# Two fields looked up by TensorE, rows fetched by SyncE, and scores in four column tiles: a change to an attention factorization machine on Trainium2

## The reference

```
B, N_DENSE, N_FIELDS, VOCAB, EMBED_DIM, ATT_DIM = (2048, 13, 26, 12500, 32, 8)
FIRST, SECOND = np.triu_indices(N_FIELDS, k=1)
emb = jax.vmap(lambda tbl, idx: tbl[idx], in_axes=(0, 1), out_axes=1)(embed_tables, sparse)
bi = emb[:, FIRST, :] * emb[:, SECOND, :]
a = jax.nn.relu(jnp.einsum('bpd,dh->bph', bi, att_w_w) + att_w_b)
scores = jnp.einsum('bph,ho->bpo', a, att_d_w) + att_d_b
att_weight = jax.nn.softmax(scores, axis=1)
att_out = jnp.sum(att_weight * bi, axis=1)
x = jnp.concatenate([att_out, dense], axis=-1)
out = jax.nn.sigmoid(x @ fin_w + fin_b)
```

## Time and profile before

| | |
|---|---|
| median of 3 executions | 534.23 us (533.74 to 535.23) |
| the profiled execution | 534.63 us, its span 532.8 us |
| POOL busy | 384.7 us (72%), 400 gathers |
| PE busy | 371.2 us (70%) |
| DVE busy | 278.7 us (52%) |
| ACT busy | 123.5 us (23%) |
| TensorE's granted clock, mean | 0.922 of full speed |

### The profile page before, as it was taken

How to read it: one execution, slowest core, us unless ns; L and a number is a source line. 1 busy time by engine, 2 the same in 40 slices (tenths; PEclk the granted TensorE clock), 3 DMA queues, 4 the chain that set the end, 5 groups by cost and what they waited for, 6 DMA issues and landing times.

```text
span 532.8 us, 6246 instructions
## 1 busy us (share of the span) xinstructions
PE 371.2 (70%) x1940; PEld 120.4 (23%) x1940; DVE 278.7 (52%) x434; ACT 123.5 (23%) x301; POOL 384.7 (72%) x404
## 2 busy tenths in 40 slices
PE   0468748788836776686946686786874678687694
PEld 0122211222312321121222221121231222112121
DVE  4144544555654455545754446455765445454674
ACT  0000012322520112222540011232442001122253
POOL 5777777777777777777777777777777777777720
PEclk9998998998969999989987999889996999788998
DMA  8223222122112222222112222322111222212210
GB/s 228 36 12 14 15 13 13 15 15 12 16 12 13 12 13 13 14 13 14 13 13 13 13 13 13 13 14 13 14 13 13 12 13 12 13 13 13 14 6 1
DMA packets 13828, 9.96 MB, mean 19 GB/s; under 512 B 6781, under 2 KB 13437, under 8 KB 13565
## 3 DMA queue, kind: packets, MB, share of 16 engines
q0 software_dynamic: 12800, 6.58, 21.1%
q1 hardware_dynamic: 730, 2.98, 2.2%
q10 hardware_dynamic: 288, 0.28, 0.2%
HBM read 9.81 MB, written 0.01 MB: 18 GB/s over the span
## 4 chain that ended last, share of the span: by engine, by line
POOL 65%; issue 21%; PE 7%; DVE 2%; DMA 2%; ACT 1%; POOLq 0%; DVEq 0%; ACTq 0%
POOL emb L250 65%; PE sums_f L303 2%; PE back_s L267 2%; PE first L294 2%; DMA emb<-tables,rows 1%; PE sums_s L314 1%; DMA par<-params 1%; ACT expd L441 0%; PE back_f L326 0%; ACT expd L415 0%; DVE onehot L506 0%; DVE second_f L551 0%; PE turned L286 0%; DVE neg_max_early L539 0%; POOLq L94 0%
## 5 line engine op out<-in xcount | busy, mean ns | idle before, releaser
L250 POOL DMA_INDIRECT emb<-tables,rows x352 | 337.2, 958 | 107.3 <-issue 107.0
L522 DVE TENSOR_TENSOR ring<-emb_t,turned 128x512 f32<-128x512 f32 (+9 forms) x180 | 193.8, 1113 | 212.1 <-PE turned L286 190.6
L303 PE MATMUL sums_f<-ring,par 128*32 128x512 f32 (+1 forms) x672 | 163.7, 634 | 0.0
L267 PE MATMUL back_s<-onehot,look_table 125*128 125x512 f32 x200 | 106.5, 671 | 58.1 <-DVE onehot L506 58.1
L294 PE MATMUL first<-ring,par 128*32 128x512 f32 (+1 forms) x672 | 107.6, 635 | 1.7 <-DVE ring L522 1.7
L382 ACT ACTIVATE hidden<-first,par 128x512 f32<-128x512 f32 (+1 forms) x84 | 56.4, 675 | 184.2 <-PE first L294 163.4
L314 PE MATMUL sums_s<-hidden,par 128*32 128x512 f32 x168 | 91.8, 637 | 2.9 <-ACT hidden L382 2.9
L286 PE MATMUL turned<-par,emb 128*128 128x128 f32 x100 | 31.5, 320 | 85.8 <-DMA emb<-tables,rows 64.4
L375 ACT ACTIVATE emb_t<-turned 128x128 f32<-128x128 f32 x100 | 27.6, 276 | 189.2 <-DVE ring L522 175.8
L267 PEld LDWEIGHTS back_s<-onehot,look_table 125*128 125x128 f32 x200 | 38.5, 207 | 115.3 <-DVE onehot L506 88.6
L250 POOL DMA_INDIRECT emb<-tables,rows_first x48 | 47.3, 986 | 18.7 <-issue 14.3
(11 more groups left out here) (50 smaller groups left out, 89.5 us busy)
## 6 DMA issues: line engine op xcount, KB each, us to landing
emb<-tables,rows POOLq DMA_INDIRECT x352, 3.3
look_table<-tables SPq DMA_DIRECT2D x1, 1400.0 KB
look_index<-look_ids SPq DMA_DIRECT2D x1, 1024.0 KB, 8.4
emb<-tables,rows_first POOLq DMA_INDIRECT x48, 3.6
par<-params ACTq DMA_DIRECT2D x1, 265.0 KB, 3.3
ids<-sparse SPq DMA_DIRECT2D x1, 208.0 KB, 2.7
look_table<-tables SPq DMA_DIRECT2D x1, 162.5 KB
feats<-dense SPq DMA_DIRECT2D x1, 104.0 KB, 2.8
```

The source lines that it names most:

```text
L250: pool.indirect_dma_start(emb[:, f, g * D:(g + 1) * D], None, stacked, bass.IndirectOffsetOnAxis(ap=row, axis=0),).then_inc(gathered[f], 16)
L267: nc.tensor.matmul(back_s[:].rearrange("p c b -> p (c b)"), look_table[:, c, :], onehot[0:LOOK_PARTS, c % ONEHOT, :], start=c == 0, stop=c ...
L303: mm = nc.tensor.matmul(sums_f[j * TILE:(j + 1) * TILE, 0:pairs_c(gr) * P], fin[:, e, :], ring[:, gr % RING, 0:pairs_c(gr), j, :], start=e ...
L522: nc.vector.tensor_tensor(slot[:, at:at + n, :], emb_t[:, i:i + n, :], turned[f % 2][:, 0:P].unsqueeze(1).broadcast_to((P, n, P)), ALU.mul ...
```

## The change

1. **Two fields are looked up**, 6 and 15. Field 6 takes five chunks at each of fields 1 to 5, field 15 three at each of fields 6 to 13 and one at 14. `look_rows` of the second runs on VectorE between the mask of field 6 and the products of field 6. SyncE loads the second table when the first is in. TensorE waits for a table at its first look-up, and no longer ahead of its first transpose.
2. **Chunk numbers lie in PSUM**: `look_chunk` is now a view of the bank `back_f`, so the one-hots read PSUM.
3. **Six tiles of field 21 are fetched by SyncE**, one row at a time (128 rows a tile, 768 transfers). It loads 16 row numbers into registers, issues 16 transfers of one row, and waits at a tile's end. One tile each for quads 0 and 1, two each for quads 2 and 3. The rows go to `emb_placed`, and ScalarE copies them into `emb` ahead of its work on field 20. GpSimd fetches the other two tiles of the placed ones at field 13 of the first quad.
4. **Scores in batches**: the score products of up to four groups stand together, each in its own column tile. Batches end at groups 3, 7, 11, 15, 17, 18 and 20. Groups lie in the banks in another order (`place`).
5. **The last field**: transpose, then first products, scores and finals of groups 18 to 20 in a written-out order; scores go back before finals.
6. `RING` 10 to 6, `HIDDEN` 4 to 6.

```diff
-RING = 10
-HIDDEN = 4
-LOOK = 10
+RING = 6
+HIDDEN = 6
+BATCH = 4
+ROWS_SP = 16
+SP_FIELD = 21
+TILES_SP = (1, 1, 2, 2)
+PLACED = 2
+SP_PLACE = 20
+SP_FIRST = 13
+LOOK = (6, 15)
+LOOK_STEP = (5, 3)
-LOOK_STEP = 3
...
+    looks_of = {f: [] for f in range(F)}
+    for n, (end, step) in enumerate(zip(LOOK, LOOK_STEP)):
+        start = LOOK[n - 1] if n else 1
+        assert (end - start) * step >= LOOKS
+        for c in range(LOOKS):
+            looks_of[start + c // step].append((n, c))
...
+    batch_ends = [gr for gr in range(GROUPS) if gr == GROUPS - 1 or
+                  gr % BATCH == BATCH - 1 and gr < FULL * GROUPS_B or
+                  gr > FULL * GROUPS_B and gr in (GROUPS - 4, GROUPS - 3)]
...
+    def place(gr):
+
+        return gr % BATCH * 2 + gr % GROUPS_B // BATCH
...
+        look_chunk = back_f[:].rearrange("p c b -> p (c b)")
...
+            stacked = tables.rearrange("f v d -> (f v) d")
+            sp.wait_ge(sp_rows_ready, 1)
+            tiles = 0
+            for q in range(QUADS):
+                for i in range(PLACED - TILES_SP[q], PLACED):
+                    t = q * G + G - PLACED + i
+                    for p in range(0, P, ROWS_SP):
+                        _, at = nc.values_load_multi_w_load_instructions(
+                            sp_rows[t:t + 1, p:p + ROWS_SP], engines=(mybir.EngineType.SP,), min_val=0,
+                            max_val=F * V - 1, skip_runtime_bounds_check_because="rows are clamped to their table")
+                        for k in range(ROWS_SP):
+                            sp.dma_start(emb_placed[p + k:p + k + 1, q, i * D:(i + 1) * D],
+                                         stacked[bass.ds(at[k], 1), :]).then_inc(sp_gathered, 16)
+                    tiles += 1
+                    sp.wait_ge(sp_gathered, tiles * P * 16)
+                sp.sem_inc(sp_quads_ready, 1)
...
-                def score_products(gr):
-                    n, c = gr // GROUPS_B, gr % GROUPS_B // 2
-                    pe.wait_ge(relu_done, q * GROUPS + (gr + 1))
+                def score_products(batch):
+                    first_gr, end = batch_ends[batch - 1] + 1 if batch else 0, batch_ends[batch]
+                    n = first_gr // GROUPS_B
+                    pe.wait_ge(relu_done, q * GROUPS + (end + 1))
...
+                    for gr in range(first_gr, end + 1):
+                        tile, half = place(gr) // 2, place(gr) % 2
+                        cut = slice(0, pairs_c(gr) * P)
+                        mm = nc.tensor.matmul(sums_s[tile * TILE:(tile + 1) * TILE, cut], d_sel[:, half, :],
+                                              hidden[:, gr % HIDDEN, cut], start=half == 0,
+                                              stop=half == 1 or gr >= FULL * GROUPS_B, skip_group_check=True)
+                    mm.then_inc(scores_done, 1)
...
+                transpose_step(F - 1)
+                score_products(BATCHES - 3)
+                first_products(GROUPS - 3)
+                final_products(GROUPS - 3)
+                score_products(BATCHES - 2)
+                first_products(GROUPS - 2)
+                first_products(GROUPS - 1)
+                final_products(GROUPS - 2)
+                score_products(BATCHES - 1)
+                final_products(GROUPS - 1)
+                scores_back(FULL)
                 finals_back(FULL)
-                scores_back(FULL)
...
+                def place_rows():
+                    act.wait_ge(placed_gathered, (QUADS * PLACED - sum(TILES_SP)) * 16)
+                    act.wait_ge(sp_quads_ready, q + 1)
+                    of_quad = emb_placed[:].rearrange("p q d -> p (q d)")[:, bass.ds(q * (PLACED * D), PLACED * D)]
+                    nc.scalar.activation(emb[:, SP_FIELD, PLACED_COLS], of_quad, ACT.Copy).then_inc(placed, 1)
...
+                    if f + 1 in LOOK:
+                        n = LOOK.index(f + 1)
+                        mask_looked(n)
+                        if n + 1 < len(LOOK):
+                            look_rows(n + 1)
```

More of the change, by code:

```diff
@@ L162, in attention_fm @@
         rows_ready = sem("rows_ready")
+        sp_ids_in = sem("sp_ids_in")
+        sp_steps = sem("sp_steps")
+        sp_rows_ready = sem("sp_rows_ready")
+        sp_gathered = sem("sp_gathered")
+        sp_quads_ready = sem("sp_quads_ready")
+        placed_gathered = sem("placed_gathered")
+        placed = sem("placed")
         gathered = [sem(f"gathered{f}") for f in range(F)]
         transposed = sem("transposed")
-        look_table_in = sem("look_table_in")
-        look_index_in = sem("look_index_in")
+        look_table_in = [sem(f"look_table_in{n}") for n in range(len(LOOK))]
+        look_index_in = [sem(f"look_index_in{n}") for n in range(len(LOOK))]
         look_steps = sem("look_steps")
@@ L242, in _ @@
                         pool.wait_ge(rows_ready, 1)
+                    if q == 0 and f == SP_FIRST:
+                        for n in range(QUADS):
+                            for i in range(PLACED - TILES_SP[n]):
+                                t = n * G + G - PLACED + i
+                                pool.indirect_dma_start(
+                                    emb_placed[:, n, i * D:(i + 1) * D], None, stacked,
+                                    bass.IndirectOffsetOnAxis(ap=rows[:, t, SP_FIELD:SP_FIELD + 1], axis=0),
+                                ).then_inc(placed_gathered, 16)
                     if q:
                         pool.wait_ge(transposed, (q - 1) * F + f + 1)
-                    for g in range(G):
+                    for g in range(G - PLACED if f == SP_FIELD else G):
                         if q == 0 and f < FIRST_FIELDS:
@@ L280, in transpose_step @@
                 def transpose_step(f):
-                    if f == LOOK:
-                        return select_step()
-                    pe.wait_ge(gathered[f], (q + 1) * (16 * G))
+                    if f in LOOK:
+                        return select_step(LOOK.index(f))
+                    pe.wait_ge(gathered[f], (q + 1) * (16 * (G - PLACED if f == SP_FIELD else G)))
+                    if f == SP_FIELD:
+                        pe.wait_ge(placed, q + 1)
                     if f >= 2:
@@ L338, in _ @@
                 transpose_step(1)
-                for f in range(1, F):
+                for f in range(1, F - 1):
                     done = groups_of(f)
                     for gr in done:
-                        if gr == done[-1] and f + 1 < F:
-                            for c in looks_of(f):
-                                look_up(c)
+                        if gr == done[-1] and f + 1 < F - 1:
+                            for n, c in looks_of[f]:
+                                look_up(n, c)
                             transpose_step(f + 1)
                         first_products(gr)
-                        if gr:
-                            score_products(gr - 1)
+                        if gr - 1 in batch_ends:
+                            score_products(batch_ends.index(gr - 1))
                         final_products(gr)
@@ L353, in _ @@
                             scores_back(gr // GROUPS_B - 1)
-                    if not done and f + 1 < F:
-                        for c in looks_of(f):
-                            look_up(c)
+                    if not done:
+                        for n, c in looks_of[f]:
+                            look_up(n, c)
                         transpose_step(f + 1)
-                score_products(GROUPS - 1)
+                transpose_step(F - 1)
[9 more added lines that the diff above has]
+                scores_back(FULL)
                 finals_back(FULL)
-                scores_back(FULL)
         @block.scalar
@@ L400, in finals_home @@
                     whole = GROUPS_B if n < FULL else END_GROUPS - 1
-                    mv = nc.scalar.activation(pairs_of(final, n * GROUPS_B, whole), finals_in_bank(0, whole), ACT.Copy)
+                    mv = nc.scalar.activation(pairs_of(final, n * GROUPS_B, whole),
+                                              finals_in_bank(every if n < FULL else end_whole), ACT.Copy)
                     if n == FULL:
                         end = final[:, :, (GROUPS - 1) * PAIRS_G:].rearrange("p g (c j) -> p g c j", j=COL_TILES)
-                        mv = nc.scalar.activation(end, finals_in_bank(whole, 1)[:, 0, :, 0:LAST_C, :], ACT.Copy)
+                        mv = nc.scalar.activation(end, finals_in_bank(end_last)[:, 0, :, 0:LAST_C, :], ACT.Copy)
                     mv.then_inc(final_done, 1)
```

142 lines of the change are left out of this document (83 added, 59 removed).

## The result

The changed kernel takes **589.1 us** (median of 4 runs, 582.77 to 590.84) against 534.05 for the kernel before: a ratio of 1.10, 95% interval [1.0963, 1.1038]. The forecast was 574 in a range of 545 to 625. The profiled execution has a span of 586.9 us.

What follows compares the result with a forecast made beforehand. The prediction took each quad's chain through TensorE and VectorE, 138.4 us against GpSimd's 118, as the bound. Start 17.2, first quad 131.9, three of 138.4 and end 7.5 gave span 571.8, forecast 574 us, range 545 to 625.

Steps and rivals of the forecast that it cites:

- own chain: Time a quad would take without waits for gathered rows: forecast to rise from 108.2 to 138.4 us, above GpSimd's 118.
- rival 1: GpSimd stays the bound because all added TensorE waits are hidden: quad chain 121, kernel 506 us; chance 0.07.
- rival 2: SyncE's rows come late, ScalarE waits at field 20 of the last quad: 664 us, half-way 618; chance 0.14.
- (c): At field 6, VectorE's row work for the second field makes TensorE idle about 5.2 us instead of 1.5: +3.7.
- (e): At fields 10 to 14 TensorE now waits for one-hots; with 0.5 for fields 7 to 9, +7.4 us a quad.
- rival 3: Half the new TensorE-VectorE turns are hidden, costing 7 instead of 14.3: quad chain 131.2, kernel 545 us; chance 0.08.
- rival 4: Four batched score products don't overlap, 3.4 us instead of 0.88: quad chain 145.6, kernel 603 us; chance 0.05.
- (a): 25 more look-ups on TensorE in each quad, 0.89 us each: +22.3 us.
- (b): One-hots read chunk numbers in PSUM, delaying TensorE 0.2 us in each turn; fields 2 to 5: +0.8 us.
- (d): After the idling at field 6, TensorE's look-ups run at a lower granted clock: +2.1 us a quad.
- (g): Batched score products save 11.2 us a quad on TensorE; 4 come back in fields 15 to 24, as VectorE limits.
- The base of 108.2: Starting point of the quad sum: the old kernel's third quad, 124.7 us, without its 16.5 us wait for gathered rows.

Runs made afterwards that it cites:

- e2: The changed kernel with one looked-up field (10, three chunks a field) instead of two; 521.4 us, ratio 0.976 to the kernel before.
- e3: The changed kernel with VectorE making a field's one-hots ahead of its wait for the transpose, not after the products; 512.5 us.
- e8: The kernel before, with one-hots made ahead of the wait for the transpose and nothing else changed; 534.5 us, ratio 1.001.
- e4: The changed kernel with the chunk numbers in SBUF instead of PSUM; 573.9 us, ratio 1.073 to the kernel before.
- e5: The changed kernel with one score product after each group (19 and 20 still together) instead of batches; 593.0 us.
- e1: The changed kernel with all tiles of field 21 fetched by GpSimd and no one-row transfers by SyncE; 585.1 us.

## Why the prediction was right, point by point

- **The mechanism held.** A quad's own chain became longer than GpSimd's 118 us, and GpSimd's saving was hidden. e2 (without the second set), e3 (without the turns) and e8 (without the turns where GpSimd binds) show the three sides of it.
- **The rivals.** The quads are 143.5 us apart and not 118 (rival 1), no engine waits for SyncE's rows (rival 2), and the waits of (c) and (e) count in full (rival 3). Four score products start 0.85 us before what follows them (386.65 to 387.50), no more than one took before, so they overlap, against rival 4; but its other half, a lower clock, is what came: 0.90 in the third quad where it was 0.93.
- **GpSimd, 94 gathers a quad, through at 481 us:** 477.6 measured, 3 us earlier; the sum had left out that one-hots from PSUM don't slow the gathers (e4).
- **(a) look-ups:** 4.41 us for five in e3, 0.88 each against 0.89.
- **(b) PSUM source:** taken 0.2 us, measured 0.25 (742 ns against 491), e4: 12 us of waits against 11.
- **(c) field 6:** 5.2 us of idling forecast, 5.12 measured.
- **(d) the clock after it:** 2.1 taken, 2.27 measured (5.11 for 2.84). But two more dips in each quad from the second on were not in the sum, at field 13 (2.7 us with what follows) and in the last field (1.6).
- **(e) turns at fields 10 to 14:** forecast 2.2, 0.5, 0.65, 2.6, 0.9; measured 2.39, 0.67, 0.74, 2.79 and none for the last, since at field 14 a batch of scores stands ahead of the look-up too.
- **(g) scores** is the step that was mis-sized. Forecast -7.2 net a quad; at an equal clock it was -3.9 (e5, first and third quad). Of the 11.2 saved on TensorE 7.3 came back, not 4, and a little more than my bound of 7: TensorE's waits in the third quad are 35.0 us with batches and 30.4 with single scores, 4.6 more, and the rest is not placed. VectorE is close to the bound of fields 15 to 24: in the changed kernel its products of two fields stand 0.34 us apart, for ScalarE's copy of the field before.

```profile
412.24 3.15 DVE L637 TENSOR_TENSOR ring<-emb_t,turned 128x1152 f32<-128x1152 f32 x2 [0.34 <-ACT emb_t L470]
```

- **The base of 108.2** was too long. I had taken the waits for rows out of the quad and left in the clock dips behind two of them. The kernel before: a field with its group after a wait of 3.1 us for rows, one after 2.9, and one without a wait.

```profile
332.10:336.60 4.50, 4.41 (x19) 0.92 (x19) 2.08 (x2) 0.96 (x2) 3.58 (x4) 0.67 0.29 13
347.80:352.20 4.40, 4.37 (x20) 1.06 (x20) 2.48 (x2) 0.69 (x1) 3.18 (x5) 0.67 0.09 11
325.70:328.70 3.00, 3.00 (x21) 0.82 (x20) 2.11 (x3) 1.24 (x3) 2.27 (x3) 1.00 0.23 13
```

That is 2.9 us that a chain without these waits doesn't have.
- **Where the 15 us are.** The start was 1.4 us later (18.6 instead of 17.2; the transposes waited for gathered rows and not for the table, as the earlier trace rows already says), the end 1.4 shorter. The first quad took 131.4 us where 131.9 was forecast, the other three 143.6 instead of 138.4: 5.2 x 3 = 15.6 us. In the third quad the terms give +3.3 for (g), +2.7 and +1.6 for the two new dips, +0.6 for the deeper dips at fields 1 and 6 and -2.9 for the base, together 5.3 of the 5.1 measured. So the good hit in the first quad was luck: (g) and the base were off by 3 us each, in opposite directions, and the new dips were not there. Why the dips came and went stays open.
- **SyncE:** 0.507 us a row against 0.6 taken and a limit of 0.64. The lower bound, 0.46 on its own queue, was nearer than my middle. The page Runtime: NRT & Kernel Launch of the Trainium skill gives about 200 ns for each register loaded, section Instruction fetch mechanics; worked out from it, a row would take 0.66, an estimate. The page speaks of loads from HBM, and these are from SBUF: the 0.507 leaves at most 0.05 for each register, so for these loads the measurement decides against it.
- **RING and HIDDEN:** no wait for a ring slot is in the trace of the changed kernel.

## What to carry to other kernels

Before a bound is lowered, work out how far below it the next one lies: here GpSimd's 126 us a quad covered a chain of 108, and a change that took 8 us from the one and added 35 to the other lost. A chain worked out by taking waits away still holds the slow stretch that followed them: read the granted clock behind each wait before it is taken out. A chain that passes back and forth between two engines isn't seen in their busy shares (TensorE 73%, VectorE 66%); it is seen in short waits of each for the other, once per step, and it may fall to a change of order that costs nothing. Measure such an edit where it binds: one-hots ahead gave 0 in the kernel before, 77 us in the changed one.

## What the runs showed of the hardware

- GpSimd's gathers slow down beside VectorE's one-hots from SBUF and not beside those from PSUM: 1.10 us for a gather that overlaps one-hots in e4 against 0.94 for one that doesn't, 976 against 946 ns in the mean of e4 and the changed kernel, 12 us in 378 gathers. The page VectorE: DVE Perf Modes of the Trainium skill, section Why PSUM operands drop a tier, says that the fast fp32 mode uses both SBUF read ports and PSUM has one; the one-hots' 491 ns from SBUF and 742 from PSUM agree. That GpSimd is held up by just this was not tested apart.
- SyncE issues transfers of one row, their address from a register, every 0.507 us, loads of 16 registers and waits included, and this slowed the other engines by at most 4 us in 589 (e1).
- The mean granted clock differed from kernel to kernel (0.90 to 0.95), and the same wait of 2.79 us was followed by look-ups at about half speed in three quads of the changed kernel and at full speed in its first; the same holds of a wait of 2.56 us in the last field. What decides it stays open.
